# Attention over pairs of query tiles, values applied right behind the scores, and a feed-forward stage two chunks deep, in a one-core macaron block

## What is computed

```python
x = x + 0.5 * ffn(layernorm(x))
x = x + attention(layernorm(x))
x = x + 0.5 * ffn(layernorm(x))
```

## Time and profile before

| what | value |
|---|---|
| median of 3 runs | 1634.21 us (1634.13 to 1634.35) |
| the profiled execution | 1628.43 us, of it 1626.6 us span of the core |
| TensorE busy, share of the span | 88% |
| GpSimd, VectorE, ScalarE busy | 61%, 60%, 48% |
| mean granted clock of TensorE | 0.976 |

### The profile page before, as it was taken

One profiled execution on the slowest core, in us unless ns is written; L12 is line 12 of the kernel. 1 busy time (PEld: TensorE's weight loads), 2 busy tenths in 40 slices (PEclk: granted clock), 3 DMA queues, 4 the chain that ended last, 5 costly groups with the idle time before them and its releaser, 6 DMA issues.

```text
span 1626.6 us, 38540 instructions
## 1 busy us (share of the span) xinstructions
PE 1439.0 (88%) x13330; PEld 1113.7 (68%) x13330; DVE 970.6 (60%) x1886; ACT 776.3 (48%) x1827; POOL 990.7 (61%) x592
## 2 busy tenths in 40 slices
PE   4767999999999999999999999999999999998676
PEld 3543777777777777777777777777777777777566
DVE  5653666666666666566666656666666656665444
ACT  2323555555555455554555555555555455454332
POOL 2231767677666667666676766677666666667410
PEclk9995999999999999999999999999999999999978
DMA  3100000000000000000000000000000000000000
GB/s 96 36 0 18 19 19 19 18 18 18 18 18 18 13 5 18 18 18 18 18 18 18 18 18 18 18 18 18 18 18 18 18 1 17 18 0 1 1 26 26
DMA packets 30571, 29.42 MB, mean 18 GB/s; under 512 B 6993, under 2 KB 25298, under 8 KB 30546
## 3 DMA queue, kind: packets, MB, share of 16 engines
q1 hardware_dynamic: 30546, 29.09, 5.9%
HBM read 8.07 MB, written 2.10 MB: 6 GB/s over the span
## 4 chain that ended last, share of the span: by engine, by line
PE 55%; issue 17%; DVE 13%; POOL 7%; ACT 6%; DVEq 1%; DMA 1%; ACTq 0%; POOLq 0%; SPq 0%
PE banks L773 16%; PE banks L754 15%; PE banks L789 8%; PE banks L719 6%; POOL probs L324 6%; ACT probs L389 5%; DVE probst L549 4%; DVE negmax L537 4%; PE banks L655 4%; PE banks L742 2%; PE banks L723 2%; DVE hidden L492 1%; PE banks L734 1%; POOL rstd_ln L295 1%; DVE xn_ln L478 1%
## 5 line engine op out<-in xcount | busy, mean ns | idle before, releaser
L324 POOL TENSOR_SCALAR probs<-probs,recips 128x704 f32<-128x704 f32 (+7 forms) x512 | 947.6, 1864 | 452.5 <-DVE recips L542 452.5
L537 DVE TENSOR_REDUCE negmax<-banks 128x1 f32<-128x704 f32 (+7 forms) x512 | 392.6, 808 | 129.8 <-PE banks L754 129.8
L773 PE MATMUL banks<-ident,probs 128*128 128x128 f32 x2752 | 391.4, 281 | 43.2 <-DVE probst L549 22.6
L397 ACT ACTIVATE probst<-banks 128x512 f32<-128x512 f32 (+1 forms) x320 | 177.4, 555 | 516.2 <-PE banks L773 516.2
L389 ACT ACTIVATE probs<-banks,negmax 128x704 f32<-128x704 f32 (+7 forms) x512 | 397.2, 785 | 44.5 <-DVE negmax L537 44.5
L773 PEld LDWEIGHTS banks<-ident,probs 128*128 128x128 f32 x2752 | 293.2, 141 | 130.3 <-issue 69.3
L549 DVE COPY probst<-banks 128x512 f32<-128x512 f32 (+1 forms) x416 | 276.6, 665 | 171.8 <-PE banks L773 169.8
L789 PE MATMUL banks<-probst,vs 128*64 128x128 f32 x5504 | 357.0, 277 | 0.8 <-ACT probst L397 0.8
L789 PEld LDWEIGHTS banks<-probst,vs 128*64 128x64 f32 x5504 | 295.3, 137 | 37.6 <-issue 22.5
L754 PE MATMUL banks<-kt,qt 64*128 64x512 f32 (+4 forms) x2496 | 298.3, 365 | 3.1 <-issue 3.1
L754 PEld LDWEIGHTS banks<-kt,qt 64*128 64x128 f32 x2496 | 206.0, 186 | 50.5 <-issue 5.8
(11 more groups left out here) (58 smaller groups left out, 881.1 us busy)
## 6 DMA issues: line engine op xcount, KB each, us to landing
hslot<-h_sb SPq DMA_DIRECT2D x32, 512.0 KB, 3.2
wslot<-in_wqkvt SPq DMA_DIRECT2D x32, 128.0 KB, 3.0
wslot<-wq_sb SPq DMA_DIRECT2D x32, 64.0 KB, 2.6
y<-xres SPq DMA_DIRECT2D x8, 256.0 KB, 2.3
wo_sb<-in_wot SPq DMA_DIRECT2D x1, 512.0 KB
wq_sb<-in_wqkvt SPq DMA_DIRECT2D x1, 512.0 KB
bslot<-bqk_sb SPq DMA_DIRECT2D x32, 1.0 KB, 1.9
iload<-in_wgatet SPq DMA_DIRECT2D x1, 192.0 KB, 2.4
```

The costliest lines, as they stand in the source:

```text
L324: nc.gpsimd.tensor_scalar(here, here, recips[:, c, h:h + 1], None, ALU.mult).then_inc(normed.sem, 1)
L397: nc.scalar.activation(probst[c % 2][:, 4 * g:4 * g + w, :].rearrange("p t q -> p (t q)"), banks[:, TRANSPOSED[g % 2], 0:w * P], ACT.Copy) ...
L537: nc.vector.tensor_reduce(negmax[:, c, h:h + 1], src, AX.X, ALU.max, negate=True).then_inc(maxed.sem, 1)
L773: last = nc.tensor.transpose(banks[:, TRANSPOSED[g % 2], (t - 4 * g) * P:(t - 4 * g + 1) * P], probs[c, h][:, kb * P:(kb + 1) * P], ident[:])
```

## The change

The attention now handles its values in pairs of query tiles. `probst` holds both tiles of a pair side by side, and `attend` runs once for a pair p (steps 2p and 2p+1) with 256 columns for each matmul. It runs in four steps, `ATTEND_AT`: pair 0 in step 5, pair 1 in step 7, pair 2 in step 1 and pair 3 in step 3 of the next turn; there it stands right behind the scores, and all transposes of that step behind it. Transposes now lag three steps. ScalarE copies the even groups and VectorE the odd ones. In the four steps with values ScalarE copies group 0 after the exponentials and after the attention result, in the others before the exponentials. The jobs are placed anew: o1 and k1 in step 0, o2 and q1 in step 2, o3 and v0 in step 4, v1 in step 5, o0, k0 and q0 in step 6; only k0 and q0 are made a turn ahead. The first two jobs of a step stand between groups 1 and 2 of its transposes, a third behind group 3.

The feed-forward stages are unrolled, with two buffers for `xth`, `hidden` and `xn_ln1`; the down projection lags one chunk, the second layernorm and the small network two or three; GpSimd normalises for the first layernorm. The first projections k0 and q0 are made at the end of stage a, the input is loaded in three parts with the first chunk ahead of everything, and in stage d VectorE makes the statistics of the first three chunks before the last copies of the attention.

Cut to its core:

```diff
-    T_LAG, PV_LAG = 2, 3
+    T_LAG, PV_LAG = 3, 5
-    JOBS = {0: ["k0"], 1: ["o2", "q0"], 2: ["k1"], 3: ["o3", "q1"], 4: ["v0"], 5: ["o0"], 6: ["v1"], 7: ["o1"]}
+    ATTEND_AT = {5: 0, 7: 1, 1: 2, 3: 3}
+    JOBS = {0: ["o1", "k1"], 1: [], 2: ["o2", "q1"], 3: [], 4: ["o3", "v0"], 5: ["v1"], 6: ["o0", "k0", "q0"], 7: []}
...
-            def attend(c, i, r):
+            def attend(p, i, r):
...
-                for kb in range(blocks[c]):
+                for kb in range(blocks[c1]):
+                    q = slice(0 if kb < blocks[c0] else P, 2 * P)
                     for h in range(2):
-                        last = mm(banks[half(h), ATTEND, 0:P], vs[r][:, kb, half(h)], probst[c % 2][:, 2 * kb + h, :],
-                                  start=(kb == 0), stop=(kb == blocks[c] - 1), skip_group_check=True)
+                        last = mm(banks[half(h), ATTEND, q], vs[r][:, kb, half(h)], probst[p % 2][:, 2 * kb + h, q],
+                                  start=(kb == 0), stop=(kb == blocks[c1] - 1), skip_group_check=True)
...
                 score(c, i, r)
+                if attending:
+                    attend(ATTEND_AT[c], *((i, r) if c >= PV_LAG else (i - 1, 1 - r)))
                 if turning:
                     turns_of(tc, ti, (0, 1))
-                for job in JOBS[c]:
-                    if job[0] == "o":
-                        do(job)
-                if attending:
-                    attend(ac, ai, r if c >= PV_LAG else 1 - r)
+                for job in JOBS[c][:2]:
+                    do(job)
                 if turning:
                     turns_of(tc, ti, (2, 3))
-                for job in JOBS[c]:
-                    if job[0] != "o":
-                        do(job)
+                for job in JOBS[c][2:]:
+                    do(job)
```

The order of ScalarE in a step, and that of VectorE:

```diff
-                if turning and groups[tc] > 1:
-                    take(tc, 1, ti)
-                if here:
-                    exps(c, i)
-                if carry or c >= PV_LAG:
-                    attention_out(ac, ai)
-                if turning and groups[tc] > 3:
-                    take(tc, 3, ti)
+                if turning and c not in ATTEND_AT:
+                    take(tc, 0, ti)
+                exps(c, i)
+                if c in ATTEND_AT and (carry or c >= PV_LAG):
+                    attention_out(ATTEND_AT[c], i if c >= PV_LAG else i - 1)
+                if turning and c in ATTEND_AT:
+                    take(tc, 0, ti)
+                if turning and groups[tc] > 2:
+                    take(tc, 2, ti)
...
                 row_max(c, i)
-                if turning:
-                    take(tc, 0, ti)
-                for job in JOBS[c]:
-                    if job[0] == "o" and (carry or job in ("o0", "o1")):
-                        add_output(job, job_turn(job, c, i))
-                if turning and groups[tc] > 2:
-                    take(tc, 2, ti)
+                if turning and groups[tc] > 1:
+                    take(tc, 1, ti)
+                for job in JOBS[c][:1]:
+                    evict(job, i, r, carry, more)
+                if turning and groups[tc] > 3:
+                    take(tc, 3, ti)
                 invert(c, i)
...
+                for job in JOBS[c][1:]:
+                    evict(job, i, r, carry, more)
```

And the order of TensorE in a feed-forward stage:

```diff
+            def feed_forward(ph):
+                transposed(ph, "ln1", 0)
...
+                for t in range(CHUNKS + 3):
+                    if t < CHUNKS:
+                        gate_up(ph, t)
...
+                    if ph is pa and 0 <= t - 3 < CHUNKS:
+                        outer(t - 3)
+                    if t + 1 < CHUNKS:
+                        transposed(ph, "ln1", t + 1)
+                    if 0 <= t - 1 < CHUNKS:
+                        down(ph, t - 1)
+                    elif ph is pa and 0 <= t - 2 < CHUNKS:
+                        transposed(pa, "ln2", t - 2)
+                        for name, bank in FIRST:
+                            project(name, 0, 0, bank)
+                    if ph is pa and 0 <= t - 2 < CHUNKS:
+                        inner(t - 2)
```

More of the change, by code:

```diff
@@ L228, in _ @@
                 sp.dma_start(dst, src).then_inc(ints_loaded, 16)
[L229 to L234, removed]
+            for k in (1, 2):
+                sp.dma_start(resident[:, x_parts[k], :], x_src[:, x_parts[k], :]).then_inc(x_loaded[k], 16)
             for dst, src in (
@@ L309, in _ @@
[L309 to L317, removed]
+                nc.gpsimd.tensor_scalar(veps[ln][:], mv[ln][t % 3][:, :, 1], EPS, None, ALU.add).then_inc(ph.rstd[ln].sem, 1)
@@ L347, in silus @@
[L347 to L358, removed]
@@ new lines, in step @@
+            def step(c, i, r, carry=True, more=True):
+                ti, tc = back(i, c, T_LAG)
+                turning = carry or c >= T_LAG
+                if turning and c not in ATTEND_AT:
[7 more added lines that the diff above has]
+                    take(tc, 2, ti)
+                for job in JOBS[c]:
+                    if job[0] in "kq" and runs(job, carry, more):
+                        queries_keys(job, job_turn(job, i), 1 - r if job_turn(job, 0) else r)
@@ L650, in down @@
[L650 to L652 removed]
+                        done(pe, ph.hid, f"h{j - HB}", t - 1)
+                    mm(banks[:, 1 + j, :], wff[:, j, :], xth[t % 2][:, 0, :], start=True, stop=False)
+                    mm(banks[:, 1 + j, :], wff[:, j, :], xth[t % 2][:, 1, :], start=False, stop=True).then_inc(ph.gu.sem, 1)
+            def down(ph, t):
+                done(pe, ph.hid, f"h{HB - 1}", t)
+                done(pe, ph.x1, "x", t - 1)
@@ L692, in _, with project @@
-            pe.wait_ge(pa.h.sem, pa.h.before("h", t - 1))
-            transposed(pa, "ln2", t - 1)
-            mlp1(t - 1)
-            down(pa, t)
-            mlp2(t - 1)
-            pe.wait_ge(pa.h.sem, pa.h.before("h", t))
-            transposed(pa, "ln2", t)
-            mlp1(t)
-            mlp2(t)
+            def project(name, n, r, bank=MISC):
+                kind, j = name[0], int(name[1])
+                if name == "k0":
+                    pe.wait_ge(slots.sem, slots.after("b", n))
+                w = wslot[r][:, "qkv".index(kind), :]
+                bank = banks[:, bank, :]
+                if kind != "v":
+                    last = mm(bank, w, hslot[r][:, j * BANK:(j + 1) * BANK], start=True, stop=True)
+                else:
+                    for m in range(4):
+                        toks = slice((4 * j + m) * P, (4 * j + m + 1) * P)
+                        last = mm(bank[:, m * P:(m + 1) * P], hslot[r][:, toks], w, start=True, stop=True)
+                last.then_inc(proj.sem, 1)
```

570 lines of the change are left out of this document (279 added, 291 removed).

## The result

The changed kernel takes 1742.03 us (median of 4 runs, 1741.77 to 1746.81), the kernel before 1634.17 us beside it: a ratio of 1.0673, 95% interval 1.0648 to 1.0699. That is 108 us more, where 32 were forecast, with the range ending at 1712. The sign was right; the size lies outside the range, nearest to the rival in which the clock falls in every turn (1728).

What follows compares the result with a forecast made beforehand. Attention was taken as bound by TensorE's order, the feed-forward stages by a chain of engines. Stage a -48.8, first turn +0.8, turns 30 x 3.7, last turn and tail +8.3, stage d -39.5 gave +31.8: 1666 us, range 1620 to 1712.

Steps and rivals of the forecast that it cites:

- the rival in which the clock falls in every turn: Step 6's waits bring TensorE to its low clock, slowing q0 and step 7's scores: 2.0 us a turn, 1728 us; chance 0.13.
- The stage sums: Scores begin at 98.6 us instead of 147.4, last turn and tail 62.6 instead of 54.3, stage d 56.8 instead of 96.3.
- Wide values: In attention, a 256-column value instruction costs 0.113 us, between 0.107 and 0.119; 9.7 us a turn instead of 10.2.
- The rival of cheap wide values: In attention, a wide value instruction may cost 0.085 us: 1.6 us a turn less, 1618 us; chance 0.12.
- The waits: TensorE waits 8.8 us a turn: step 6 1.85 and 2.0, step 4 1.25, step 2 0.75, step 0 0.85, step 7 1.5, others less.
- the walk's 46.7: Length of an attention turn from walking its eight steps one by one: 46.7 us, 3.7 us longer than before.
- the price of a projection: TensorE's time for one projection from start to start, taken as 0.86 us.
- turn 0 was given +0.8 us: k1, q1, v0 and v1 move into the first attention turn, whose 37.2 us become 38.
- The comparison that misled: Argument against the clock rival: the first stage has such gaps mostly at the full clock.
- The sign: Whole kernel: slower with chance 0.82, faster 0.15, same 0.03.

Runs made afterwards that it cites:

- both holes filled: Changed kernel with two unread 512-column matmuls ahead of k0 and two ahead of q0 in step 6; 1675.94 us, ratio 1.0261.
- k0 early: Changed kernel with the next turn's k0 made in step 3 instead of step 6; median 1634.09 us, ratio 1.0013.
- order back: Changed kernel with transposes before values and ScalarE's copy before the exponentials in the four steps with values; 1704.31 us; with k0 in step 3 too, 1571.89 us.
- addition first: Changed kernel with VectorE adding an output before copying group 1; 1672.98 us; with k0 early and order back too, 1534.10 us.
- The same loop, behind a longer program: Attention of the kernel before, with its own jobs, between the changed kernel's feed-forward stages; 1662.46 us, ratio 1.0183.

## Why the prediction was wrong, point by point

- **The stage sums** held: a 99.84 us against 98.6, d 55.80 against 56.8 (whose terms, as written, add up to 56.6), tail 63.05 against 62.6. Both feed-forward stages are bound by TensorE, as costed, at clocks of 0.97 and 0.99. A chunk takes 8.1 us (8.3 forecast) and 5.9 us (6.0), and TensorE has no gap in the middle of either: it is busy for all of the 24.20 us from 47.50 to 71.70 and of the 29.60 us from 1697.20 to 1726.80.
- **Wide values.** Forecast 0.113 us each. The 32 instructions of pair 3, in step 3 of the turn above, take 458.22 - 454.62 = 3.60 us from start to start, 0.1125 each, after 59.4 ns for one of 128 columns before. The rival of cheap wide values (0.085) fell: twice the columns take 1.9 times as long, so 80 instructions fewer a turn, 2560 in all, brought next to nothing.

```profile
454.62 3.67 PE L829 MATMUL banks<-probst,vs 128*64 128x256 f32 x32
458.22 0.65 PE L813 MATMUL banks<-ident,probs 128*128 128x128 f32 x4
```

- **The waits.** 1.85 and 1.84 us in step 6, 1.19 in step 4, 0.72 and 0.67 to 0.81 in steps 2 and 0, each released by VectorE's addition or eviction as written. The wait of step 7 is 1.32 where the clock is full, against 1.5. With both holes filled the turn is 47.13, 0.43 over the walk's 46.7. Undoing the waits took the turn to 45.0 (k0 early), 43.6 (order back) and 42.6 (addition first) at the full clock, each within 0.2 us of its sum.
- **The step that failed** is the weighing of the rival "the clock falls in every turn", at a chance of 0.13. The forecast added up waits at a clock of 1.00 and kept the fall as an unlikely rival, on the ground that stage a has such gaps at the full clock. The traces show it in each of the thirty turns. Filling the two holes, and nothing else, gives back 1.0 us in step 6 and 1.1 in step 7 (means over the turns): 2.15 a turn, 64 of the 82 us by which the profiled span missed. The rival had the mechanism and the price (2.0) nearly right; its chance was too low.
- **Two smaller terms.** The walk itself was 0.43 us a turn too short, 13 us in thirty turns; a part of that is the price of a projection, 0.86 for 0.96 where one starts behind a wait. And turn 0 was given +0.8 us for the jobs that move into it, while the waits that the same prediction had found in steps 6 and 7 were put at nothing there. These two steps take 10.1 and 8.2 us in turn 0, after 6.1 and 5.7 in the kernel before, and 9.2 and 6.8 with the holes filled: 4.5 us of the miss.
- **The comparison that misled** was with stage a, whose waits before were 1.5, 0.7 and 1.1 us, shorter than step 6's and with a matmul of the small network between them; and even there the granted clock of the stage was 0.89. The nearer row was the one of stage d in the earlier trace rows. The Trainium skill, TensorE: Matmul & The Clock Gate, HAM oscillation, describes waits that recur with each tile and throttle TensorE each time. The turns agree with it now, 49.28 us against 47.13 with the holes filled; the waits of the page's kernel are waits for DMA and longer than the 1.85 and 1.84 us here.
- **The sign.** The one rival that would have made the kernel faster, cheap wide values, fell. The change was slower for its job table and its orders: the same tiling, buffers and feed-forward stages with three edits of the order are 6% faster than before, and k0's move alone brings 4.0 of the 6.7 us a turn between the changed kernel and that one.

## What to carry to other kernels

Cost a hole on TensorE twice: once as the wait, and once as what may follow at the low clock. Here 3.7 us of holes in step 6 were followed by 2.15 us more, and one such hole was at times enough. When an order is written by hand, a job that shares one bank with the job before it must have other work of its engine between them, and that work must be longer than the reader's queue (here two maxima, a copy and an addition). Where a wait can't be removed, filling it with idle matmuls shows in one run what the clock takes: 66 us here.

## What the runs showed of the hardware

- The clock fell behind waits of under 2 us. By the turns of one execution each: in all thirty with holes of 1.85 and 1.84 us in step 6; in 16 with the first alone (1.87), in 9 with the second alone (1.84), in 14 with 1.27 and 1.84, in five and in four with a single hole of 1.77; never with both filled (longest hole left 1.33) and never with a longest hole of 1.18. The two ends are clear; the order of the counts between them is not shown, since the runs of one kernel differ.
- The same loop, behind a longer program, stood still for 4.8 to 5.8 us in each of fourteen rounds and moved 145 instruction packets instead of 15. With 128 instructions more ahead of it, 73 packets and six rounds with a stall of 4.4 to 4.6 us were left.
- Eight transposes have 1.02 us to the next start ahead of values and 0.93 ahead of other work, in the changed orders too (433.53 to 434.55 and 439.44 to 440.37 in the kernel with the order back). That the 0.1 us is the change of the array's layout, 128 columns of weights for transposes and 64 for values, is the likely cause; no run separates it from others.
